# Opening of an adaLN transformer block: x by batch, query-key columns first, exp table loaded at once, weight split in two parts

## The reference, cut to what matters

```python
mod = (_silu(L0_c) @ L0_wmod).reshape(8, 6, 1, -1)
sa, ca, ga, sb, cb, gb = (mod[:, i] for i in range(6))
h = _layernorm(x, axis=-1) * (1 + ca) + sa
qkv = h @ c_attn_w + c_attn_b            # 256 x 768
Q, K, V = jnp.split(qkv, 3, axis=2)
# two softmaxes over Q K^T (the first on 128 of 256 dims; its context gives,
# through tanh(ctx * cam_gate), a bias of the second), context @ c_proj_w
x = x + ga * attention
h = _layernorm(x, axis=-1) * (1 + cb) + sb
x = x + gb * (routed experts(h) + shared expert(h))
```

## Time and profile before

| | us |
|---|---|
| median of 3 runs | 285.05 (284.52 to 286.57) |
| the profiled execution | 288.81 |
| its span, first to last instruction | 286.9 |
| TensorE busy in it | 261.6 (91%) |
| TensorE's mean granted clock | 0.982 of full speed |

### The profile page before, as it was taken

One profiled execution on the slowest core, in us unless ns is written; L12 is line 12 of the kernel. 1 busy time (PEld: TensorE's weight loads), 2 busy tenths in 40 slices (PEclk: granted clock), 3 DMA queues, 4 the chain that ended last, 5 costly groups with the idle time before them and its releaser, 6 DMA issues.

```text
span 286.9 us, 6248 instructions
## 1 busy us (share of the span) xinstructions
PE 261.6 (91%) x1836; PEld 242.4 (84%) x1836; DVE 195.0 (68%) x593; ACT 161.3 (56%) x429; POOL 127.5 (44%) x146
## 2 busy tenths in 40 slices
PE   1799999898999999999999759999999999999980
PEld 1797788897889999888989659989999999999980
DVE  2675875038988672786488746464788857868876
ACT  2437568878467574838336562455656556565530
POOL 3120313754172058858990844600545445444460
PEclk9999999999999999999999968999999999999997
DMA  7894006333331113232170223434753338475745
GB/s 237 277 345 108 0 9 220 95 103 104 103 100 59 37 39 111 75 98 91 45 235 3 75 74 127 155 90 123 201 161 108 121 108 282 151 256 169 208 130 195
DMA packets 29671, 37.50 MB, mean 131 GB/s; under 512 B 4308, under 2 KB 24255, under 8 KB 29640
## 3 DMA queue, kind: packets, MB, share of 16 engines
q1 hardware_dynamic: 25144, 28.24, 33.3%
q0 software_dynamic: 3216, 8.46, 7.9%
q10 hardware_dynamic: 1280, 0.41, 0.6%
HBM read 24.78 MB, written 12.71 MB: 131 GB/s over the span
## 4 chain that ended last, share of the span: by engine, by line
PE 76%; issue 6%; ACT 5%; DMA 4%; DVE 4%; POOL 3%; ACTq 1%; SPq 1%; DVEq 0%; POOLq 0%
PE bank L345 18%; PE bank L347 17%; PE bank L346 16%; PE bank L1140 4%; PE bank L1355 3%; PE bank L1377 3%; PE bank L1112 3%; PE bank L1132 2%; PE bank L1095 2%; PE bank L1123 2%; PE bank L1104 2%; DMA mh<-routed_out 1%; PE bank L1013 1%; DMA routed_out<-yo_all,dest 1%; DMA h2all<-routed_in 1%
## 5 line engine op out<-in xcount | busy, mean ns | idle before, releaser
L1482 POOL DMA_INDIRECT routed_out<-yo_all,dest x35 | 35.2, 1005 | 51.5 <-ACT yo_all L1426 34.7
L345 PE MATMUL bank<-experts_w,h2T_lo 128*128 (+1 forms) x156 | 50.6, 324 | 0.0
L347 PE MATMUL bank<-experts_w,h2T_hi 128*128 (+1 forms) x156 | 47.2, 303 | 0.0
L346 PE MATMUL bank<-experts_w,h2T_hi 128*128 (+1 forms) x156 | 47.0, 301 | 0.0
L708 POOL DMA_INDIRECT routed_in<-h2all,slot_u x32 | 31.7, 991 | 25.7 <-DVE slot_u L689 14.3
L345 PE MATMUL bank<-h2T_hi,wsgu_lo 128*128 128x256 f32 (+1 forms) x96 | 29.1, 303 | 2.9 <-issue 2.9
L346 PEld LDWEIGHTS bank<-experts_w,h2T_hi 128*128 128x128 f32 (+1 forms) x156 | 29.7, 190 | 0.0
L345 PEld LDWEIGHTS bank<-experts_w,h2T_lo 128*128 128x128 f32 (+1 forms) x156 | 29.6, 190 | 0.0
L347 PEld LDWEIGHTS bank<-experts_w,h2T_hi 128*128 128x128 f32 (+1 forms) x156 | 29.3, 188 | 0.0
L347 PE MATMUL bank<-h2T_hi,wsgu_hi 128*128 128x256 f32 (+1 forms) x96 | 28.1, 293 | 0.0
L346 PE MATMUL bank<-h2T_lo,wsgu_hi 128*128 128x256 f32 (+1 forms) x96 | 28.0, 292 | 0.0
(11 more groups left out here) (270 smaller groups left out, 780.8 us busy)
## 6 DMA issues: line engine op xcount, KB each, us to landing
h2all<-routed_in SPq DMA_DIRECT2D x39, 130.0 KB
wstage<-gu_t SPq DMA_DIRECT2D x8, 352.0 KB
res<-x SPq DMA_DIRECT2D x4, 512.0 KB, 9.1
mx<-modrow SPq DMA_DIRECT2D x8, 256.0 KB, 3.6
mh<-modrow SPq DMA_DIRECT2D x8, 256.0 KB
exchange<-routed_out SPq DMA_DIRECT2D x8, 256.0 KB
wmod_s<-w_mod SPq DMA_DIRECT2D x3, 512.0 KB, 10.0
out<-res SPq DMA_DIRECT2D x6, 256.0 KB
```

The lines of the kernel that those rows point to most:

```text
L345: pe.matmul(out_ap, l[1], r[0], start=start, stop=False)
L346: pe.matmul(out_ap, l[0], r[1], start=False, stop=False)
L347: return pe.matmul(out_ap, l[0], r[0], start=False, stop=stop)
L1482: pool.indirect_dma_start(out=routed_out, out_offset=bass.IndirectOffsetOnAxis(dest[:, t % 16:t % 16 + 1], 0), in_=yo[t % 6], in_offset=No ...
```

## The change

The opening is ordered anew.

- SP: `sp_setup` now loads x of batch 0 alone, the first third of the modulation weight, the 512 query-key columns of `w_qkv`, x of batch 1 alone (semaphore `xb1_in`), the 256 value columns, `w_proj` (both on `wproj_in`), then the rest of the modulation weight.
- ScalarE: behind the DMA of c stands an exp of a constant into a cell that is overwritten later; the exp of c is moved in front of the last three small DMAs. The hi part of the query-key weight is made in two parts (m = 0, 1), that of the value columns (`act_wcam`) behind `act_h(0)`, waiting for value columns and `w_proj`. The copies of batch 0's first half of the product come before `act_h(1)`.
- VectorE: statistics of batch 0, silu, statistics of batch 1, normalise 0, sacol, lo part 0, column constants, lo part 1, h(0), and only then normalise 1.
- GpSimd: the power is taken for batch 0, for batch 1, for the pair 2 and 3, and for 4 to 7.
- TensorE: modcol, transposes of batch 0, first half of batch 0's product, transposes of batch 1 and of the value weight, second half, s1(0), fold. `pe_spin` is called with a count of 0 and issues nothing.
- The shared expert's down weight shares the semaphore of the other late weights.

```diff
@@ SP
+                sp_first_x(sp, 0)
+                sp_mod(sp, 0, s_wmod0_in)
+                sp.dma_start(q3[:, :, 0:2 * D], qkv[:, :, 0:2 * D]).then_inc(s_wqkv_in, 16)
+                sp_first_x(sp, 1)
+                sp.dma_start(q3[:, :, 2 * D:], qkv[:, :, 2 * D:]).then_inc(s_wproj_in, 16)
+                sp.dma_start(p3, w_proj.rearrange("(k p) n -> p k n", p=P)).then_inc(s_wproj_in, 16)
+                for j in range(1, MCH):
+                    sp_mod(sp, j, s_wmod_in)
...
+            def sp_first_x(sp, b):
+                sp.dma_start(res[:, b], x_in[b].rearrange("(t p) d -> p t d", p=P)).then_inc((s_x0_in, s_xb1_in)[b], 16)
@@ ScalarE
                 act.dma_start(cT[:], c_t.rearrange("(k p) b -> p k b", p=P)).then_inc(s_c_in, 16)
+                act.wait_ge(s_const, 1)
+                act.activation(lw[:, 5:6], minus_half[:, 0:1], ACT.Exp)
                 act.dma_start(cols[:, 0:3 * KD], b_cols).then_inc(s_cols_in, 16)
                 act.dma_start(cols[:, 3 * KD:3 * KD + 1], gate_col).then_inc(s_cols_in, 16)
+
+                act.wait_ge(s_c_in, 16)
+                act.activation(cS[:], cT[:], ACT.Exp, scale=-1.0).then_inc(s_c_exp, 1)
                 act.dma_start(lw[:, 0:1], cam_w0.partition_broadcast(P)).then_inc(s_cols_in, 16)
                 act.dma_start(lw[:, 1:2], cam_w1.partition_broadcast(P)).then_inc(s_cols_in, 16)
                 act.dma_start(bprow[:], b_proj.partition_broadcast(B)).then_inc(s_cols_in, 16)
...
                 act.wait_ge(s_wqkv_in, 16)
-                act.activation(wqk[0][:], q3[:, :, 0:2 * D], ACT.Copy).then_inc(s_whi, 1)
+                for m in range(KD):
+                    act.activation(qk_part(wqk[0][:], m), qk_part(q3, m), ACT.Copy).then_inc(s_whi, 1)
...
                     act_h(act, 0)
+                    act_wcam(act)
+                    act.wait_ge(s_cols_ready, 3)
+                    act_qk(act, 0, 0)
                     act_h(act, 1)
                     act_lw(act)
                     act_fold(act)
-                    act.wait_ge(s_cols_ready, 3)
-                    act_qk(act, 0, 0)
                     act_qk(act, 0, 1)
@@ VectorE
+            LN1 = ((0,), (1,), (2, 3), (4, 5), (6, 7))
...
+                    dve_ln1_stats(dve, 0)
                     dve_silu(dve)
-                    dve_ln1_stats(dve, 0)
+                    dve_ln1_stats(dve, 1)
                     dve_normalise(dve, 0)
+                    dve_sacol(dve)
+                    dve_wqk(dve, 0)
+                    dve_cols(dve)
+                    dve_wqk(dve, 1)
+                    dve_h(dve, 0)
                     dve_normalise(dve, 1)
-                    dve_wqk(dve)
-                    dve_sacol(dve)
-                    dve_cols(dve)
-                    dve_h(dve, 0)
                     dve_wcam(dve)
-                    dve_ln1_stats(dve, 1)
                     dve_h(dve, 1)
+                    dve_ln1_stats(dve, 2)
@@ TensorE
+                    pe_spin(pe, 0)
                     pe_modcol(pe)
                     pe_xt(pe, 0)
+                    pe_spin(pe, 0)
+                    pe_qk(pe, 0, (0,))
                     pe_xt(pe, 1)
                     pe_fold_in(pe)
-                    pe.wait_ge(s_wlo, 1)
-                    pe_qk(pe, 0)
+                    pe_qk(pe, 0, (1,))
+                    pe_s1(pe, 0)
                     pe_fold(pe)
-                    pe_s1(pe, 0)
                     pe_qk(pe, 1)
```

More of the change, by code:

```diff
@@ L497, in pool_rstd2, with dve_stats @@
             pool_rstd(pool, s_var2, p + 1, mv2[:, :, 1], rs2[:], s_rstd2, 2 * p)
-        def dve_stats(dve, p, bst, mv, spare, stats, var, at):
-            for b, u in pair_of(p):
+        def dve_stats(dve, batches, nth, bst, mv, spare, stats, var, at):
+            for u, b in enumerate(batches):
                 for t in range(TT):
@@ L503, in dve_stats @@
             last.then_inc(stats, 1)
-            dve.wait_ge(stats, 2 * p + 1)
+            dve.wait_ge(stats, 2 * nth + 1)
             dve.memset(spare[:], 0.0).then_inc(stats, 1)
-            for j in range(at, at + 2 * TT):
+            for j in range(at, at + len(batches) * TT):
                 last = dve.bn_aggr(mv[:, j, :], bst[:, j, :])
@@ L812, in sp_setup, with sp_mod @@
             def sp_setup(sp):
[L813 to L817, removed]
+                qkv = w_qkv.rearrange("(k p) n -> p k n", p=P)
+                sp_first_x(sp, 0)
[6 more added lines that the diff above has]
+                    sp_mod(sp, j, s_wmod_in)
+            def sp_mod(sp, j, into):
+                sp.dma_start(wmod_s[:, :, ms(j)], w_mod[:, ms(j)].rearrange("(k p) n -> p k n", p=P)).then_inc(into, 16)
+            def sp_first_x(sp, b):
+                sp.dma_start(res[:, b], x_in[b].rearrange("(t p) d -> p t d", p=P)).then_inc((s_x0_in, s_xb1_in)[b], 16)
             def sp_x(sp, first, after, into):
@@ L997, in dve_later_down, with pe_spin @@
                                              ALU.mult, ALU.subtract).then_inc(s_wlo_later, 1)
+            def pe_spin(pe, times):
+                for _ in range(times):
+                    pe.matmul(HB[1][:, 0:P], ident[:], ident[:], start=True, stop=True)
             def pe_modcol(pe):
@@ L1065, in pe_qk @@
                     pe.wait_ge(s_qk_second, b)
-                for m, to in enumerate(QK):
+                for m in ms:
+                    to = QK[m]
+                    pe.wait_ge(s_wlo, 1 + m)
                     for half in range(2):
@@ L1656, in _ @@
                     pool_setup(pool)
-                    pool_rstd1(pool, 0, 1)
-                    pool_rstd1(pool, 1, 2)
-                    pool_rstd1(pool, 2, 4)
+                    pool_rstd1(pool, 0, 0, 0)
+                    pool_rstd1(pool, 1, 1, 1)
+                    pool_rstd1(pool, 2, 2, 2)
+                    pool_rstd1(pool, 3, 3, 4)
                     pool_rows(pool)
```

53 lines of the change are left out of this document (27 added, 26 removed).

## The result

The kernel after takes 289.94 us (median of 4 runs, 288.56 to 290.37), the kernel before 285.81 beside it (4 runs, 284.52 to 287.96): ratio 1.0123, 95% interval 1.0085 to 1.0161. By the ratio that is 3.5 us slower, by the two medians 4.1, and either way above the range given (283.0 to 288.0). The profiled execution took 290.0 us, span 287.7.

What follows compares the result with a forecast made beforehand. TensorE bounds the kernel nearly everywhere, so the opening pays only through its dense start and that work's cost: -0.5 us for an earlier T0, +0.93 for TensorE's order, sum +0.4, giving 285.5 us; range 283.0 to 288.0.

Steps and rivals of the forecast that it cites:

- T0: First matmul of batch 0's query-key product on TensorE: 14.65 before, forecast 14.15, ends 13.25 and 15.05.
- S: Moment compared in the experiments, not a forecast term: start of batch 1's scores on TensorE, 27.71 before, 29.39 after.
- The late fall of TensorE's clock: Rival: a small shift removes the half-clock stretch after the gap at 165 to 168 us, -2.6 us; chance 0.12.
- VectorE now asks for them only behind h(1), past 19: VectorE's opening: x(2), x(3) may land up to 1 us later, since their statistics now come after h(1).
- So the shift passes on unchanged: TensorE runs almost without idle time from 26 to 110 us, so the opening's +0.4 us reaches the total.
- I carry the difference over to it unscaled: Times from the profiled 288.81 us execution; their difference applied directly to the median of 285.05, 3.76 lower.
- its ends: Landing of x(1) in the opening's loads: 8.0 at the early end, 9.8 at the late, 8.9 taken as middle.
- The constants: Column constants VectorE reads behind sacol: small loads until about 11, T0 13.2 at the earliest; waiting past 11.5 meant wrong.
- The eight transposes between the halves: TensorE, between halves of batch 0's product: once free, now on the dense path, 1.7 us at the lower clock.
- the late-clock rival: Clock rises 5.6 us after the second half starts, not after T0: 1.9 us more, 287.4 in all; chance 0.18.
- The term for the scores in front of the fold: TensorE: batch 0's softmax can start 1.7 us sooner relative to T0, but TensorE is full there; worth nothing.
- the forecast's late end: x(1), of 1 KB rows, lands 2.8 us behind the query-key columns, at 9.8, as w_proj did behind w_qkv.

Runs made afterwards that it cites:

- Transposes in front: Kernel after with transposes of batch 1 and value weight back before batch 0's undivided product, normalise 1 behind normalise 0: 288.8 us, ratio 1.0122.
- ScalarE's order of before: Kernel after with both transposes ahead of batch 0's product and ScalarE's h(1) right behind h(0); VectorE's statistics of 2 and 3 stay behind h(1): 286.38 us, ratio 1.0011.
- ScalarE's alone: Kernel before with one ScalarE move: eviction of the first query-key half, with its wait for TensorE, in front of h(1): 283.89 us, ratio 1.0046.
- both edits together: Kernel after with all small DMAs issued before the wait for c and both transposes ahead of batch 0's product: 289.6 us, ratio 1.0145.
- only the two orders: Kernel before with ScalarE's first-half eviction in front of h(1) and VectorE's statistics of 2 and 3 behind h(1): 288.15 us, ratio 1.0107.
- small loads first: Kernel after with ScalarE's last three small loads issued ahead of the wait for c: 289.31 us, ratio 1.0124.
- the orders of before on after's loads: Kernel after with the opening's orders on TensorE, ScalarE and VectorE as in before; loads, early table, split weight, scores before fold kept: 283.8 us, ratio 1.0024.
- the statistics first: Kernel after with VectorE's statistics of batches 2 and 3 moved in front of h(1): 285.55 us, ratio 1.0091.

## Why the prediction was wrong

**The cause.** h(1) was made late on ScalarE, by standing behind the eviction of the first query-key half, which waits for TensorE; and on VectorE the statistics of 2 and 3, the layer weight, the normalise and the maximum are queued behind it. The first half of this is shown. *Transposes in front* and *ScalarE's order of before* differ in ScalarE's order alone. In both profiles TensorE's pace rises 2.9 us after T0 (T0 is 14.67 and 14.37), and S is 28.95 against 26.04: 2.9 us, of which 0.3 is T0; the ratios are 1.0122 and 1.0011. The second half, that VectorE's order makes it worse, has S and both pairs of the table for it (27.66 for both orders; 26.28 for ScalarE's alone, and there it is the wait for wvT that holds it; each at full pace from T0), but no interval that is clear of its neighbour's.

Behind S the kernels hardly differ. The profiled time less S is 258.7 to 260.1 us in the eight profiles of the first and third sets and 256.5 to 257.8 in the six of the second and fourth, while S itself lies anywhere from 24.80 to 29.57. The late fall of TensorE's clock is no rival either: on the pages of the fourteen profiles only *both edits together* and *only the two orders* have one, and ratios of 1.0122 and 1.0146 are reached without.

**The steps that failed.** There are two.

The first is in the sentence on x(2) and x(3): "VectorE now asks for them only behind h(1), past 19". The forecast saw this move and counted it as cover for a late landing. It did not follow what stands behind the statistics in turn. With h(1) at 19.9, as measured, the rest follows from times of the kernel before: 1.15 for it, 1.9 for the statistics, 1.3 for GpSimd's power, 1.3 for the normalise, maximum at 25.5, 0.7 for it, and 3.1 of ScalarE's queue from the exp to K: 29.3, with 29.39 measured. The prediction priced TensorE's order in full and ScalarE's, which the same edit changed, only by the wait for v in it. "So the shift passes on unchanged" fell with it.

The second is that the whole sum was made on one late-clock execution and then "I carry the difference over to it unscaled". On that execution the forecast was close: with the measured T0 its terms give 0.38 + 0.93 = 1.31 for the end of batch 1's product, and 1.30 was measured (25.89 to 27.19). S moved by 1.68, and the profiled time was 290.0 where 288.81 + 0.4 = 289.2 was forecast. Nor would the chain have been seen there: with the forecast's T0 of 14.15 and the eviction at 16.8 it puts S at 28.1, and TensorE's own path (product ending at 26.4, 1.8 for the row modulation) puts it at 28.2. The chain shows in full only where TensorE's pace comes up early.

**Why 3.5 us, where the two profiled executions differ by 1.2.** The profile of before was an execution of 288.81 us, 3.76 above the median that the prediction was carried over to; that of after was at its median. In the openings with before's orders TensorE's first dense work sets S. After, the chain does, of which only the start hangs on the clock. From a late rise to full pace at T0, S goes from 27.71 to 24.80 with the orders of before (the second on after's loads), 2.9 us; with both orders of after from 29.39 to 27.66 (the second on before's loads), 1.7. So at full pace the two sides differ by 27.66 - 24.80 = 2.9 us, and in the late-clock profiles by 1.7. That the difference of the medians is made up in this way is argued from these pairs, not shown.

**Point by point.** The table load ran at 1.33 and held up no issue (the next two began at 1.40 and 1.85). sacol stood ahead of the weight's lo. x(1) landed at 9.3 instead of 8.9, inside its ends, but by two errors that cancel: the query-key columns landed at 8.1 instead of 7.0, and x(1) 1.2 us behind them, not the 1.9 of the middle. The constants were mis-sized: by about 11 in the forecast, 12.94 in the trace, one of the forecast's own signs of being wrong. T0 was 15.03 instead of 14.15: 0.46 for x(1), the other 0.42 for the wait for the constants. Yet T0 did not matter: with 14.67 (transposes in front) the ratio was the same. The eight transposes between the halves took the 1.7 us foreseen, and TensorE did not stand still between the halves, so the late-clock rival in its own form is out: the pace changed at 20.75, 5.7 us after T0. The late fall of the clock stayed in the profile after, in a shorter form, about 171 to 174 instead of 168 to 174. The term for the scores in front of the fold, nothing, and the loads as a whole hold: 1.0024 for the two with the rest. By the Trainium skill ("DMA: Bandwidth & Descriptors", Specifications), which gives 512 B as the least size for full rate, the 1 KB rows of x(1) would not be slowed. The traces are nearer to that than to the forecast's late end: in the eight profiles that load x(1) behind the query-key columns it came 0.7 to 1.2 us behind them in seven, close to the 1.0 of the early end, and 2.5 in one (*small loads first*). What set that one apart is not known.

## What to carry to other kernels

When an edit moves an instruction on one engine, write out the queue of every engine that consumes it and follow what is behind the consumer, to the end of the chain, with the trace's own times; a stage that only gets "asked for later" is a cost until its followers have been priced. Engines with idle time ahead of them in the profile (2.20 us ahead of the maximum here) lend cover only as long as their own inputs come on time. And before a bound is given away, ask which engine it belongs to, and whether the profile at hand is a typical execution: an opening bound by TensorE gained 2.9 us from an early clock here, one bound by a chain across three other engines 1.7, and a sum made on a late-clock profile hides the difference.

## What the runs showed of the hardware that was not expected

The moment at which TensorE's pace goes from 0.21 to 0.12 us per 256-column matmul differs between executions of nearly the same opening. Two kernels of one set, the first dense matmul within 0.05 us of each other; first the orders of before on after's loads, then the statistics first:

```profile
14.46 0.39 PE L345 MATMUL bank<-hT_hi,wqk_lo 128*128 128x256 f32 x1 [0.74 <-DVE hT_lo L1250]
14.68 0.28 PE L346 MATMUL bank<-hT_lo,wqk_hi 128*128 128x256 f32 x1
14.80 0.28 PE L347 MATMUL bank<-hT_hi,wqk_hi 128*128 128x256 f32 x1
```

```profile
14.51 0.58 PE L345 MATMUL bank<-hT_hi,wqk_lo 128*128 128x256 f32 x1 [2.66 <-DVE hT_lo L1250]
14.89 0.41 PE L346 MATMUL bank<-hT_lo,wqk_hi 128*128 128x256 f32 x1
15.11 0.41 PE L347 MATMUL bank<-hT_hi,wqk_hi 128*128 128x256 f32 x1
```

The first is at 2.4 GHz at once, the second at 1.2 GHz until about 20.6. The idle time in front differs (0.74 and 2.66), but *transposes in front* also had 0.74 and stayed at the slow pace for 2.9 us. The kernel before had 1.46 in front and the slow pace for 5.6 us, and both kernels with only orders moved had 1.46 too, the same list on TensorE up to there, and the full pace. Over all sixteen profiles the rise comes between 0 and 6.1 us after T0. What decides is open. For a forecast it means that one profile of a short opening can be off by up to 2.5 us, an estimate from 5.6 us at the lower pace, each worth 0.44.

The small loads of ScalarE's queue are slow by time, not by bytes: the last, 8 KB, was issued at 5.73 and released VectorE only at 12.94, 7.2 us later, and in the five other profiles where VectorE stood for it, it took 7.2 to 8.5 us from its issue. Whether issuing them sooner delays the loads beside them can't be told: x(1) came at 10.07 in one kernel with that edit and at 9.14 in the other, against 9.36 after.
